# Extra steps of an attention stage at other places in five engines' orders

## The chip, the cores and the metric

The kernel runs on one core of one Trainium2 chip. The metric is the device time of one execution in microseconds (us). An execution that the hardware profiler records has a time of its own; the profile and the trace below are of that one execution. Engines: PE is TensorE, DVE is VectorE, ACT is ScalarE, POOL is GpSimd, SP is SyncE, which here only issues DMAs. Each engine works through a queue of its own in order; they are tied together by semaphores alone.

## The reference

For x of 8 sequences x 256 tokens x 512 features, all in float32:

```
x = x + stack(layernorm(x))        # projection to 64, 4 layers of convolution and a small MLP, projection to 512
x = x + ffn(layernorm(x))          # 512 -> 1792 (gate, up) -> 512, weights w * (su @ sv), SiLU
x = x + attention(layernorm(x))    # below
x = x + ffn(layernorm(x))          # the same weights again
```

The attention has 32 heads of 128 in 8 groups of 4 that share one key and value head:

```
q, k, v = x @ Wq.T, x @ Wk.T, x @ Wv.T            # per head
q, k = rmsnorm(q), rmsnorm(k)
scores = q @ k.T / sqrt(128) + slope[head] * (key - query)   # causal: later keys get -1e30
out = softmax(scores) @ v                          # per head
return concat(out) @ Wo.T
```

## The kernel before

Everything is written by hand for the five queues. Three phases follow one another; the change touches the second, the attention (`order2` and the functions that carry it out), and not the planners of the first and third.

**Units.** The attention stage has 64 units, one per group g (0 to 7) and sequence b (0 to 7), u = 8 g + b. Unit u attends: scores (`sc`, 4 heads), bias and maximum (`bias`, DVE), exponential (`exp`, ACT), reciprocal sum (`rsum`, DVE), scaling of the probabilities (`norm`, POOL, L2446), transposes (`pT`, PE), their split into a high and a low part (`pThi` ACT L2395, `pTlo` DVE L2551), values (`at`), split of the output (`oThi`, `oTlo`, L2556), output product (`outa`, `out`) and residual sum into x (`oadd`, DVE L2561). Beside it the same unit makes q, k and v of unit u + 1: seven products (`qkv`, a Strassen-like scheme), their sums on DVE (`u2` L2455, `u3`, `c22`, `c11`, `u4`, `c21`, `c12`, one semaphore `c_done`), squares (ACT), the inverse roots (`nrm`, POOL L2414), scaling (`ksc` ACT, `qsc1` POOL L2418, `qsc0` DVE L2489), v's split (`vhi`, `vlo` L2486), transposes of k and q (`kT`, `qT`) and their splits (`qTlo` L2527, `kTlo` L2522). The next unit's `sc0` waits for `kTlo` and `qTlo`.

**Order.** Each engine's order within a unit is a line of names, `UNIT_STEPS` (L1946). Besides these steps some units have extra ones. Names such as `set0`, `set1`, `sums`, `rows` in the lines are places for them, and `besides` (L1960) says which extra step stands at which place in which unit:

- **Statistics** `ln` (3, tile): bn_stats and bn_aggr (`dve_ln`, L1374 and L1377) of the tiles of x that earlier units have finished, for the layer norm of the last phase. Two tiles at DVE's `set1` in units 57 to 60, that is (7,1) to (7,4).
- **Sets of weights.** For each group the q, k, v weights are needed in seven parts: three are quarters of the raw weights, four are sums. For group g + 1 they are made in group g, for g = 1 to 6. SP fetches the raw weights at `set0` of b = 1 (`qf`, L912). POOL makes the four sums at `sums` of b = 2 to 5 (`qcomb`, lines 866 to 878 in `pool_group`), 128 x 768 each, from SBUF to SBUF. ACT writes each part's high half (`qhi`, L892) and DVE its low half (`qlo`, L897, two inputs in SBUF): in b = 2, 3, 4 an even part at `set0` and an odd one at `set1`, in b = 5 the seventh at `set1`. SP saves both halves to DRAM (`qsv`, L916). There is a single buffer `q_parts2`, so each `qhi` waits for the save before it. ACT's `set0` stands ahead of its first `exp`.
- **Last sequences' rows.** The normalised, transposed rows of sequences 6 and 7 and the sums of their quarters are made in group 0: `arow` (DVE), `axT` (PE transposes), `aev` (ACT), `acomb` (POOL, four sums, L1007 to L1012) in unit q - 3, then `ahi` (ACT), `alo` (DVE, L965) and the save `asv` (SP) in unit q - 2. The transposes borrow the PSUM banks of k and q, hence the waits of `pe_sequence` on `c_done` and of `kT` and `qT` on `aev`.

SP loads the next rows' operands (`lx`, `xs<-weff_x`, L2265) at `set0`, behind the save that stands at `sets0`; the load waits for the products of the unit (`qkv_mm`).

Of the kernel before, what the change touches and what calls it, by code (L numbers as in the profile page):

```python
# [15 lines left out]
BATCH, SEQ, DM = 8, 256, 512  # L16
# [13 lines left out]
STILES = SEQ // P  # L30
SC = P + SEQ
UNITS = KVH * BATCH
# [136 lines left out]
def hybrid_block(nc, x_in, win, vecs, b1, w1, w2, wout, bout, ffn_w, lr_long, lr_short, wqkv, wo, qk_w, out, weff_gu, weff_dn, weff_s, weff_q, weff_x):  # L169
    with ExitStack() as ctx:  # L170
# [17 lines left out]
        pe, act, dve, pool, sp = nc.tensor, nc.scalar, nc.vector, nc.gpsimd, nc.sync  # L188
# [779 lines left out]
        def pe_sequence(q, j):  # L968
            if q < SEQS1:
                wait_bank(("axT", q, j))  # L970
            else:

                pe.wait_ge(c_done, summed(q - 2, ("c11", "c21")[j]))
            bank, row = sequence_bank(q, j), sequence_row(q, j)
            pe.wait_ge(a_dve, A_DVE["arow", q, j])
            for k in range(KC):
                ins = pe.transpose(psum[:, bank, k * P:(k + 1) * P], row[:, k * P:(k + 1) * P], ident[:])
            ins.then_inc(a_tile, 1)
# [910 lines left out]
        def sb2(name, shape, dt=F32):  # L1889
# [56 lines left out]
        UNIT_STEPS = {  # L1946
# [13 lines left out]
        def besides(engine, where, u):  # L1960

            g, b = divmod(u, BATCH)
            steps = []

            if where == "set0" and engine == "act" and b == 0:
                steps += [("swo", g, 0), ("swo", g, 1)]
            if where in ("set0", "sums") and engine == "pool" and b == 0:
                steps.append(("swo", g, 0 if where == "set0" else 1))
            if where in ("set0", "set1") and engine == "dve" and b == BATCH - 1 and g + 1 < KVH:
                steps += [("alibi", g + 1, hd) for hd in ((0, 1) if where == "set0" else (2, 3))]  # L1970

            if where == "set1" and engine == "dve":
                if UNITS - 7 <= u < UNITS - 3:
                    steps.append(("ln", (3, STILES * (u - UNITS + 7)), STILES))
            if where in ("set0", "set1") and engine == "dve" and u == 0:
                first_tile = NT - TPB + (2 if where == "set1" else 0)
                steps.append(("ln", (2, first_tile), 2))
            if engine == "pool":
                if where == "sums" and u == 1:
                    steps.append(("inv", 2, NBLK - 1))  # L1980
                if where == "set1" and u in (UNITS - 6, UNITS - 4):
                    steps.append(("inv", 3, (u - UNITS + 6) // 2))

            later_g = g + MADE_AHEAD
            if g and later_g < KVH and b in range(2, 6):
                half = 1 if where[-1] == "1" else 0
                e = 2 * (b - 2) + half if b < 5 else 6
                if where in ("set0", "set1", "sets0", "sets1") and engine in ("act", "dve", "sp") and (b < 5 or half) and \
                        (engine == "sp") == where.startswith("sets"):
                    steps.append(({"act": "qhi", "dve": "qlo", "sp": "qsv"}[engine], later_g, e))  # L1990
                if where == "sums":
                    steps.append(("qcomb", later_g, b - 2))

            fresh = u + 3
            if SEQS1 <= fresh < BATCH:
                steps += {("dve", "set0"): [("arow", fresh, 0)], ("pe", "rows"): [("axT", fresh, 0)],
                          ("act", "rows"): [("aev", fresh, 0)], ("dve", "rows"): [("arow", fresh, 1)],
                          ("pe", "set1"): [("axT", fresh, 1)], ("act", "set1"): [("aev", fresh, 1)],
                          ("pool", "set1"): [("acomb", fresh, 0)]}.get((engine, where), [])
            fresh = u + 2  # L2000
            if SEQS1 <= fresh < BATCH and where in ("set0", "rows", "set1") and engine in ("act", "dve"):
                steps.append(({"act": "ahi", "dve": "alo"}[engine], fresh, ("set0", "rows", "set1").index(where)))
            if SEQS1 <= fresh < BATCH and where == "sets1":
                steps.append(("asv", fresh, 0))

            if engine == "sp" and where == "set0":
                if b == BATCH - 2 and g + 1 < KVH:
                    steps += [("lqw", g + 1, j) for j in range(7)] + [("lwo", g + 1, 0)]
                if u + 3 < UNITS and u + 3 not in range(SEQS1, BATCH):
                    steps.append(("lx", u + 3, 0))  # L2010
                if g and later_g < KVH and b == 1:
                    steps.append(("qf", later_g, 0))
                if u == UNITS - 4:
                    steps.append(("load", 0, 0))
            return steps

        def unit_steps(engine, u):
            for name in UNIT_STEPS[engine].split():
                if name in SUMS2:
                    step_ = ("sum", u + 1, name)  # L2020
                elif name in ("set0", "set1", "sums", "rows", "sets0", "sets1"):
                    if u >= 0:
                        yield from besides(engine, name, u)
                    continue
                else:
                    step_ = (name[:-1], u + (name[:-1] in PROJECTING), int(name[-1]))
                assert step_[0] in PROJECTING or step_[0] in ATTENDING

                done = step_[1] == 0 and step_[0] in ("qkv", "prcopy", "sum", "sqr", "nrm", "ksc", "qsc", "vhi", "vlo")
                if 0 <= step_[1] < UNITS and not done:  # L2030
                    yield step_
# [38 lines left out]
        def summed(n, name):  # L2070
            return len(SUMS2) * n + SUMS2.index(name) + 1
# [521 lines left out]
        def pe_phase2():  # L2593
            for what, a, b in order2["pe"]:
# [5 lines left out]
                    pe_projection(a, b)  # L2600
                elif what == "kT":
                    pe.wait_ge(k_sc, a + 1)
                    if SEQS1 <= a + 2 < BATCH:
                        pe.wait_ge(a_act, A_ACT["aev", a + 2, 0])
                    pe.wait_ge(c_done, summed(a, "c11"))
                    for t in range(STILES):
                        ins = pe.transpose(psum[:, KV, t * P:(t + 1) * P], cc[:, t, 0, 0:HD], ident[:])
                    ins.then_inc(kT_mm, 1)
                elif what == "qT":
                    pe.wait_ge(q_sc1 if b else q_sc0, a + 1)  # L2610
                    if b == 0 and SEQS1 <= a + 2 < BATCH:
                        pe.wait_ge(a_act, A_ACT["aev", a + 2, 1])
                    pe.wait_ge(c_done, summed(a, "c12" if b else "c21"))
                    for hd in range(GRP):
                        ins = pe.transpose(psum[:, QB[b], hd * P:(hd + 1) * P], q_heads(b)[:, hd // 2, hd % 2, :], ident[:])  # L2615
# [329 lines left out]
```

## Time and profile before

| | |
|---|---|
| runs shown | 2433.47, 2441.58, 2434.09 us (median 2434.09) |
| the profiled execution | 2437.14 us, span 2435.8 us |
| PE busy | 2373.6 us, 97% of the span |
| DVE, ACT, POOL busy | 1646.2, 1189.8, 800.6 us |
| units of the attention stage | from 684.4 us to about 2000 us, 64 of some 20 to 23 us |
| data moved | 444.85 MB, 183 GB/s on average |

The span is the time from the first to the last instruction of the profiled execution; its own time has 1.3 us around it. Busy time is the time in which an engine carries out an instruction; register, branch, semaphore and DMA-issuing instructions do not count. A unit's length is read as the distance between two first score products (`psum<-kT,qT_h`). A row of the windows view gives a stretch of the span (from:to), its length, the busy time of PE, PEld (weight loads), DVE, ACT and POOL in it with their instructions, the granted clock of PE (1.00 is full speed), the DMA engines' share and GB/s. A row of the timeline gives start, duration, engine, line, operation, output<-inputs, shapes, and in brackets the idle time of the engine before it and what ended it.

### The profile page before, as it was taken

The page shows a single profiled execution, that of the slowest core. Times are in us where ns is not written, and L with a number is a line of the kernel's source. Part 1 is how long each engine was busy: PE and PEld are TensorE (multiplying, and loading weights), DVE is VectorE, ACT ScalarE, POOL GpSimd, SP SyncE. Part 2 cuts the span into 40 slices and gives each one's busy share as a digit, 9 for nine tenths or more (in the row PEclk, how much of TensorE's full clock was granted, in tenths as well). Part 3 has the DMA queues.
Part 4 walks back from the last instruction along what each step waited for, and adds up shares of the span by engine and source line. Part 5 has one row for each costly group of instructions (what it writes and reads, how often), then busy time and mean ns, then how long its engine had stood idle before and what let it go on. Part 6 is the DMA issues. An engine that isn't in the chain of part 4 may idle for free.

```text
span 2435.8 us, 40875 instructions
## 1 busy us (share of the span) xinstructions
PE 2373.6 (97%) x12810; PEld 2020.9 (83%) x12810; DVE 1646.2 (68%) x3961; ACT 1189.8 (49%) x3788; POOL 800.6 (33%) x1204
## 2 busy tenths in 40 slices
PE   6899999999999999999999999999999989999999
PEld 4577777788888888988989889889898878888887
DVE  7666664534277877777777777777777776565553
ACT  6433332233256666666666666666666562222112
POOL 5530343212034344444443444444434350011000
PEclk9899999999999999999999999999999999999999
DMA  4235458987830634535346335344462306555554
GB/s 144 98 134 188 185 206 293 347 334 285 313 122 31 259 118 158 213 147 198 151 173 231 121 153 212 143 183 173 169 238 92 113 19 232 195 208 185 193 193 156
DMA packets 86579, 444.85 MB, mean 183 GB/s; under 512 B 9496, under 2 KB 16664, under 8 KB 66656
## 3 DMA queue, kind: packets, MB, share of 16 engines
q1 hardware_dynamic: 85008, 440.78, 48.5%
q8 instruction: 108, 1.77, 0.3%
q10 hardware_dynamic: 1360, 1.46, 0.2%
q14 instruction: 103, 0.84, 0.1%
HBM read 342.59 MB, written 99.61 MB: 182 GB/s over the span
## 4 chain that ended last, share of the span: by engine, by line
PE 82%; DMA 7%; DVE 4%; POOL 3%; ACT 2%; issue 2%; SPq 0%; ACTq 0%; POOLq 0%; DVEq 0%
PE psum L801 70%; DMA stage<-in_wqkv 3%; PE psum L2639 3%; PE psum L2615 2%; DMA weff_s<-short_st 1%; DMA weff_q<-q_parts 1%; POOL rr L2414 1%; PE psum L2633 1%; POOL prob L2446 1%; PE psum L1793 1%; DVE cc L2489 1%; PE psum L1814 1%; POOL srstd L1184 1%; PE psum L1826 1%; ACT prob L2388 1%
## 5 line engine op out<-in xcount | busy, mean ns | idle before, releaser
L801 PE MATMUL psum<-qw,xs 128*128 128x384 f32 x2688 | 512.0, 340 | 1.7 <-DMA xs<-weff_x 1.7
L801 PEld LDWEIGHTS psum<-qw,xs 128*128 128x128 f32 x2688 | 462.3, 189 | 2.5 <-DMA xs<-weff_x 1.9
L2446 POOL TENSOR_SCALAR prob<-prob,rsum 128x128 f32<-128x128 f32 (+1 forms) x512 | 231.6, 468 | 613.3 <-DVE rsum L2548 608.2
L2388 ACT ACTIVATE prob<-biased,nmax 128x256 f32<-128x256 f32 (+1 forms) x512 | 227.3, 447 | 125.8 <-DVE nmax L2538 125.8
L801 PE MATMUL psum<-wo_h,oT_h 128*128 128x512 f32 x512 | 214.3, 419 | 0.2
L801 PE MATMUL psum<-wo_h,oT_l 128*128 128x512 f32 x512 | 202.7, 396 | 0.0
L801 PE MATMUL psum<-wo_l,oT_h 128*128 128x512 f32 x512 | 202.5, 395 | 0.0
L2334 ACT ACTIVATE squares<-cc 128x128 f32<-128x128 f32 x512 | 152.6, 302 | 52.6 <-DVE cc L2468 49.6
L2489 DVE TENSOR_TENSOR cc<-cc,rr 128x512 f32<-128x512 f32 x64 | 97.7, 1526 | 102.3 <-POOL rr L2414 102.3
L2414 POOL TENSOR_TENSOR rr<-ss,mneg_half 128x6 f32<-128x6 f32 (+1 forms) x128 | 150.3, 1174 | 10.7
L801 PE MATMUL psum<-xT0h,wgu 128*128 128x512 f32 x448 | 152.1, 399 | 0.0
L2551 DVE TENSOR_TENSOR pT_l<-psum,pT_h 128x384 fp32r<-128x384 f32 x256 | 136.1, 552 | 22.9 <-ACT pT_h L2395 15.5
L801 PE MATMUL psum<-xT1h,wgu 128*128 128x512 f32 x448 | 147.3, 394 | 0.0
L801 PE MATMUL psum<-xw_h,wS 128*128 128x512 f32 x448 | 147.1, 389 | 0.0
L2395 ACT ACTIVATE pT_h<-psum 128x384 fp32r<-128x384 f32 x256 | 113.2, 489 | 59.4 <-PE psum L2639 58.4
L801 PE MATMUL psum<-kT,qT_h 128*128 128x256 f32 x512 | 114.5, 305 | 5.6 <-DVE kT L2522 5.6
L2639 PE MATMUL psum<-ident,prob 128*128 128x128 f32 x768 | 109.1, 275 | 9.0 <-POOL prob L2446 8.8
L2556 DVE TENSOR_TENSOR oT_l<-psum,oT_h 128x512 fp32r<-128x512 f32 x128 | 87.6, 684 | 43.8 <-ACT oT_h L2400 43.4
L801 PEld LDWEIGHTS psum<-wo_h,oT_h 128*128 128x128 f32 x512 | 96.2, 188 | 23.8 <-DVE oT_l L2556 4.7
L801 PEld LDWEIGHTS psum<-wo_h,oT_l 128*128 128x128 f32 x512 | 96.2, 188 | 23.0
L1420 DVE TENSOR_TENSOR d<-gate,psum 128x512 f32<-128x512 f32 x56 | 38.4, 686 | 112.2 <-PE psum L801 75.5
L801 PE MATMUL psum<-xw_h,wA 128*128 128x512 f32 x336 | 112.7, 389 | 1.4 <-issue 1.4
(338 smaller groups left out, 5903.0 us busy)
## 6 DMA issues: line engine op xcount, KB each, us to landing
xs<-weff_x SPq DMA_DIRECT2D x62, 1792.0 KB, 7.9
wgu<-weff_gu SPq DMA_DIRECT2D x42, 1024.0 KB, 7.9
weff_q<-q_parts SPq DMA_DIRECT2D x56, 768.0 KB, 3.6
qw<-weff_q SPq DMA_DIRECT2D x56, 768.0 KB, 8.0
wD<-weff_dn SPq DMA_DIRECT2D x56, 512.0 KB, 4.7
wS<-weff_s SPq DMA_DIRECT2D x28, 1024.0 KB, 7.0
wdn<-weff_dn SPq DMA_DIRECT2D x42, 512.0 KB, 4.1
weff_gu<-wgu SPq DMA_DIRECT2D x14, 1024.0 KB, 4.2
```

What stands on the lines that cost most here:

```text
L801: ins = pe.matmul(out_ap, stat[a], mov[b], start=start and n == 0, stop=stop and n == last)
L1420: dve.tensor_tensor(F["d"][:], F["gate"][:, a % 2, :], psum[:, UP, :], ALU.mult).then_inc(d_done, 1)
L2334: ins = act.activation(squares[:, first_place + hd, :], cc[:, tile, half, (hd + 1) * HD:(hd + 2) * HD], ACT.Square, accum_out=ss[:, n:n + 1])
L2388: act.activation(prob[:, b, lo:hi], biased[:, b % 2, lo:hi], ACT.Exp, bias=nmax[:, b, t:t + 1], scale=-1.0, accum_out=esum[:, b, t:t + 1]) ...
L2395: act.activation(pT[0][:, b % 2, :], psum[:, b, 0:SC], ACT.Copy).then_inc(pT_hi, 1)
L2414: pool.tensor_tensor(rr[:, part], ss[:, part], mneg_half[:, 0:part.stop - part.start], ALU.pow).then_inc(r_done, 1)
L2446: pool.tensor_scalar(prob[:, b, lo:hi], prob[:, b, lo:hi], rsum[:, b, t:t + 1], 1.0, ALU.mult, ALU.mult).then_inc(prob_done, 1)
L2489: dve.tensor_tensor(q_heads(0), *q_scaled(0), ALU.mult).then_inc(q_sc0, 1)
L2551: dve.tensor_tensor(pT[1][:, b % 2, :], psum[:, b, 0:SC], pT[0][:, b % 2, :].bitcast(F32), ALU.subtract).then_inc(pT_lo, 1)
L2556: dve.tensor_tensor(oT[1][:, hs, :], psum[:, 2 * b, :].rearrange("p (h c) -> p h c", h=2), oT[0][:, hs, :].bitcast(F32), ALU.subtract).the ...
L2615: ins = pe.transpose(psum[:, QB[b], hd * P:(hd + 1) * P], q_heads(b)[:, hd // 2, hd % 2, :], ident[:])
L2639: ins = pe.transpose(psum[:, b, k * P:(k + 1) * P], prob[:, b, k * P:(k + 1) * P], ident[:])
```

## The change

It changes places only; no instruction is added or removed. There are two new places on DVE, `wait0` (before u2) and `wait1` (before qsc0). The statistics go there, one tile each. The even `qlo` go from `set0` (behind c21) to `wait0`. POOL's `qcomb` goes from `sums` (between norm1 and norm2) to `set0` (before norm0). The rows of sequences 6 and 7, with their transposes, evictions and sums, go one unit earlier (unit q - 4), and the waits that guard their banks with them.

```diff
--- before.py
+++ after.py
@@ -970,7 +970,7 @@
                 wait_bank(("axT", q, j))
             else:
 
-                pe.wait_ge(c_done, summed(q - 2, ("c11", "c21")[j]))
+                pe.wait_ge(c_done, summed(q - 3, ("c11", "c21")[j]))
             bank, row = sequence_bank(q, j), sequence_row(q, j)
             pe.wait_ge(a_dve, A_DVE["arow", q, j])
             for k in range(KC):
@@ -1946,8 +1946,8 @@
         UNIT_STEPS = {
             "pe": "sc0 sc1 sc2 sc3 qkv1 qkv7 qkv6 pT0 pT1 qkv5 qkv2 qkv4 at0 qkv3 rows pT2 pT3 outa0 at1 set1 outa1 kT0 qT1 qT0 "
                   "out0 out1",
-            "dve": "bias0 bias1 rsum0 bias2 rsum1 bias3 u2 pTlo0 u3 pTlo1 c22 c11 rsum2 rsum3 u4 c21 set0 oTlo0 c12 rows pTlo2 "
-                   "pTlo3 qsc0 oTlo1 set1 vlo0 qTlo1 qTlo0 kTlo0 oadd0 oadd1",
+            "dve": "bias0 bias1 rsum0 bias2 rsum1 bias3 wait0 u2 pTlo0 u3 pTlo1 c22 c11 rsum2 rsum3 u4 c21 set0 oTlo0 c12 rows "
+                   "pTlo2 pTlo3 wait1 qsc0 oTlo1 set1 vlo0 qTlo1 qTlo0 kTlo0 oadd0 oadd1",
             "act": "set0 exp0 exp1 exp2 prcopy0 pThi0 pThi1 exp3 sqr5 sqr2 oThi0 sqr4 rows pThi2 pThi3 sqr3 ksc0 oThi1 vhi0 set1 qThi1 "
                    "kThi0 qThi0",
             "pool": "set0 norm0 norm1 sums norm2 norm3 nrm1 nrm0 qsc1 set1",
@@ -1969,9 +1969,8 @@
             if where in ("set0", "set1") and engine == "dve" and b == BATCH - 1 and g + 1 < KVH:
                 steps += [("alibi", g + 1, hd) for hd in ((0, 1) if where == "set0" else (2, 3))]
 
-            if where == "set1" and engine == "dve":
-                if UNITS - 7 <= u < UNITS - 3:
-                    steps.append(("ln", (3, STILES * (u - UNITS + 7)), STILES))
+            if where in ("wait0", "wait1") and UNITS - 7 <= u < UNITS - 3:
+                steps.append(("ln", (3, STILES * (u - UNITS + 7) + int(where[-1])), 1))
             if where in ("set0", "set1") and engine == "dve" and u == 0:
                 first_tile = NT - TPB + (2 if where == "set1" else 0)
                 steps.append(("ln", (2, first_tile), 2))
@@ -1985,13 +1984,13 @@
             if g and later_g < KVH and b in range(2, 6):
                 half = 1 if where[-1] == "1" else 0
                 e = 2 * (b - 2) + half if b < 5 else 6
-                if where in ("set0", "set1", "sets0", "sets1") and engine in ("act", "dve", "sp") and (b < 5 or half) and \
-                        (engine == "sp") == where.startswith("sets"):
+                if where in {"act": ("set0", "set1"), "dve": ("wait0", "set1"), "sp": ("sets0", "sets1")}.get(engine, ()) and (
+                        b < 5 or half):
                     steps.append(({"act": "qhi", "dve": "qlo", "sp": "qsv"}[engine], later_g, e))
-                if where == "sums":
+                if engine == "pool" and where == "set0":
                     steps.append(("qcomb", later_g, b - 2))
 
-            fresh = u + 3
+            fresh = u + 4
             if SEQS1 <= fresh < BATCH:
                 steps += {("dve", "set0"): [("arow", fresh, 0)], ("pe", "rows"): [("axT", fresh, 0)],
                           ("act", "rows"): [("aev", fresh, 0)], ("dve", "rows"): [("arow", fresh, 1)],
@@ -2018,7 +2017,7 @@
             for name in UNIT_STEPS[engine].split():
                 if name in SUMS2:
                     step_ = ("sum", u + 1, name)
-                elif name in ("set0", "set1", "sums", "rows", "sets0", "sets1"):
+                elif name in ("set0", "set1", "wait0", "wait1", "sums", "rows", "sets0", "sets1"):
                     if u >= 0:
                         yield from besides(engine, name, u)
                     continue
@@ -2600,16 +2599,16 @@
                     pe_projection(a, b)
                 elif what == "kT":
                     pe.wait_ge(k_sc, a + 1)
-                    if SEQS1 <= a + 2 < BATCH:
-                        pe.wait_ge(a_act, A_ACT["aev", a + 2, 0])
+                    if SEQS1 <= a + 3 < BATCH:
+                        pe.wait_ge(a_act, A_ACT["aev", a + 3, 0])
                     pe.wait_ge(c_done, summed(a, "c11"))
                     for t in range(STILES):
                         ins = pe.transpose(psum[:, KV, t * P:(t + 1) * P], cc[:, t, 0, 0:HD], ident[:])
                     ins.then_inc(kT_mm, 1)
                 elif what == "qT":
                     pe.wait_ge(q_sc1 if b else q_sc0, a + 1)
-                    if b == 0 and SEQS1 <= a + 2 < BATCH:
-                        pe.wait_ge(a_act, A_ACT["aev", a + 2, 1])
+                    if b == 0 and SEQS1 <= a + 3 < BATCH:
+                        pe.wait_ge(a_act, A_ACT["aev", a + 3, 1])
                     pe.wait_ge(c_done, summed(a, "c12" if b else "c21"))
                     for hd in range(GRP):
                         ins = pe.transpose(psum[:, QB[b], hd * P:(hd + 1) * P], q_heads(b)[:, hd // 2, hd % 2, :], ident[:])
```

## Rows read from the trace of the kernel before

**Rows 1.** Page, busy time of each engine.

```profile
PE 2373.6 (97%) x12810; PEld 2020.9 (83%) x12810; DVE 1646.2 (68%) x3961; ACT 1189.8 (49%) x3788; POOL 800.6 (33%) x1204
```

**Rows 2.** Page, the chain that ended last, by engine.

```profile
PE 82%; DMA 7%; DVE 4%; POOL 3%; ACT 2%; issue 2%; SPq 0%; ACTq 0%; POOLq 0%; DVEq 0%
```

**Rows 3.** Windows: (0,3), (0,4), (0,5); (7,1) to (7,5); (7,5); (7,6).

```profile
749.37:770.44 21.07, 20.91 (x130) 19.12 (x128) 16.24 (x46) 14.12 (x52) 10.49 (x17) 1.00 0.00 1
770.44:793.57 23.13, 21.10 (x129) 18.96 (x128) 19.33 (x51) 15.34 (x55) 11.34 (x17) 1.00 0.08 33
793.57:814.49 20.92, 20.19 (x120) 18.41 (x121) 17.46 (x49) 13.63 (x52) 7.54 (x13) 1.00 0.45 174
...
1857.73:1961.86 104.13, 102.37 (x601) 91.26 (x600) 80.69 (x236) 62.09 (x245) 37.85 (x69) 1.00 0.23 84
...
1941.49:1961.86 20.37, 20.36 (x120) 18.41 (x121) 15.59 (x45) 12.41 (x49) 7.03 (x13) 1.00 0.02 6
...
1961.86:1982.07 20.21, 20.21 (x122) 18.29 (x120) 15.14 (x44) 12.44 (x49) 7.03 (x13) 1.00 0.08 19
```

**Rows 4.** Windows, sum over the six units b = 2 of groups 1 to 6.

```profile
sum 125.94, PE 123.34 PEld 108.85 DVE 97.61 ACT 83.50 POOL 57.75; mean PE 20.56 PEld 18.14 DVE 16.27 ACT 13.92 POOL 9.63
```

**Rows 5.** Windows, b = 3 and 4: (3,3) with (3,4); sum over six pairs.

```profile
1243.56:1284.08 40.52, 40.52 (x241) 36.51 (x241) 33.26 (x93) 27.78 (x102) 19.25 (x28) 1.00 0.44 170
...
sum 248.88, PE 245.51 PEld 218.53 DVE 199.32 ACT 166.79 POOL 115.52; mean PE 40.92 PEld 36.42 DVE 33.22 ACT 27.80 POOL 19.25
```

**Rows 6.** Timeline, kTlo at the end of (7,2); windows, (7,3).

```profile
1899.00 0.47 DVE L2522 SCALAR_TENSOR_TENSOR kT<-psum,kw,kT 128x256 fp32r<-128x256 f32 x1
...
1899.53:1920.52 20.99, 20.55 (x120) 18.24 (x120) 16.38 (x49) 12.41 (x49) 7.04 (x13) 1.00 0.25 89
```

**Rows 7.** Waits, attention stage: sum us, times, longest.

```profile
DVE cc L2489 <- POOL rr L2414: 102.3, 63, 1.7
```

**Rows 8.** Groups by form, attention stage: busy us, mean ns of one, idle before.

```profile
L1374 DVE BATCH_NORM_STATS2 ln_bn<-x 128x6 f32<-128x512 f32 x12 | 8.0, 670 | 0.0
```

**Rows 9.** Timeline, u2 of (2,3): start, us, [idle before <-releaser].

```profile
1086.14 0.55 DVE L2455 TENSOR_TENSOR su<-pr,psum 128x384 f32<-128x384 f32 x1 [0.76 <-PE psum L801]
```

**Rows 10.** Timeline, qhi of (4,4), begun 1427.76; landing of odd saves, (4,3) and (2,5).

```profile
1430.87 0.85 ACT L892 ACTIVATE q_parts<-qt 128x768 fp32r<-128x768 f32 x1 [4.91 <-DMA weff_q<-q_parts]
...
DMA to landing us min/median/max: 5.1/5.1/5.1
...
DMA to landing us min/median/max: 3.2/3.2/3.2
```

**Rows 11.** Timeline, front of (2,2): its qhi and its first norm.

```profile
1062.14 0.85 ACT L892 ACTIVATE q_parts<-stage 128x768 fp32r<-128x768 f32 x1 [4.30 <-DMA stage<-in_wqkv]
...
1064.17 0.83 POOL L2446 TENSOR_SCALAR prob<-prob,rsum 128x128 f32<-128x128 f32 x2 [8.66 <-DVE rsum L2548]
```

**Rows 12.** Timeline, first phase, qcomb and qlo beside each other.

```profile
441.11 1.86 POOL L866 TENSOR_TENSOR qt<-stage 128x768 f32<-128x768 f32 x1 [14.67 <-DMA stage<-in_wqkv]
441.94 1.83 DVE L897 TENSOR_TENSOR q_parts<-stage,q_parts 128x768 fp32r<-128x768 f32 x1 [3.41 <-ACT q_parts L892]
442.92 2.56 POOL L870 TENSOR_TENSOR qt<-stage 128x768 f32<-128x768 f32 x1
```

**Rows 13.** Timeline, end of (2,3) and the first score product of (2,4).

```profile
1095.51 1.04 POOL L2418 TENSOR_TENSOR cc<-cc,rr 128x512 f32<-128x512 f32 x1
...
1095.58 1.53 DVE L2489 TENSOR_TENSOR cc<-cc,rr 128x512 f32<-128x512 f32 x1 [1.67 <-POOL rr L2414]
...
1097.63 0.94 DVE L897 TENSOR_TENSOR q_parts<-qt,q_parts 128x768 fp32r<-128x768 f32 x1
...
1098.49 0.41 DVE L2486 TENSOR_TENSOR v_l<-cc,v_h 128x256 fp32r<-128x256 f32 x1
...
1100.03 0.47 DVE L2522 SCALAR_TENSOR_TENSOR kT<-psum,kw,kT 128x256 fp32r<-128x256 f32 x1
...
1100.67 0.41 PE L801 MATMUL psum<-kT,qT_h 128*128 128x256 f32 x2
```

## The prediction

> **What bounds the kernel now.** I read the page's busy times first: PE is busy for 97% of the span, DVE for 68%, POOL for 33% [rows 1]. The chain that ended last says the same: 82% of it is PE [rows 2]. So work taken off DVE, ACT or POOL is worth nothing by itself; only stretches in which PE waits can change. The changed steps lie in the attention stage alone. I cut it into its 64 units, written (g, b) for group and sequence, each from its first score product to that of the next. An ordinary unit lasts 20.21 us with PE busy throughout, at a granted clock of 1.00 [rows 3]. The longer ones are those with extra steps:
> - units (0,3), (0,4), (0,5), with the last sequences' rows: 21.07, 23.13 and 20.92 us [rows 3];
> - b = 2 of groups 1 to 6, with the first steps of a set of weights: 125.94 us for six [rows 4];
> - b = 3 and 4 of the same groups: 248.88 us for six pairs. An undisturbed pair takes 40.52 (two of the six do) [rows 5];
> - (7,1) to (7,4), with the statistics: with their successor (7,5) 104.13 us for five units, of which (7,5) is 20.37 [rows 3].
>
> **Part 1, statistics.** Eight bn_stats/bn_aggr pairs leave the place before vlo0, one pair each goes to wait0 (before u2) and wait1 (before qsc0). Nothing is added or removed. Today they push vlo, both qTlo and kTlo, for which the next unit's first score product waits: kTlo ends at 1899.47 and the unit begins at 1899.53, 0.06 later [rows 6]. At the new places DVE idles. Before qsc0 it waits 63 times for POOL's reciprocal roots, 102.3 us in all or 1.6 each [rows 7]. Before u2 it idled 0.76 even in a unit whose exponentials stood behind a qhi [rows 9], and these units have none. A pair is about 0.85 us (12 bn_stats take 8.0 us [rows 8], and an aggregation). Both places hold it; without that cover a pair would cost its 0.85. The gain is 104.13 - 5 x 20.21 = **3.08 us**.
>
> **Part 2, last sequences.** Rows, transposes, evictions and sums of sequences 6 and 7 go one unit earlier, to (0,2) and (0,3); their splits and saves stay in (0,4) and (0,5). So (0,4) loses its second load. Each unit then has the load of one that the trace shows: (0,2) and (0,3) that of today's (0,3), 21.07; (0,4) and (0,5) that of today's (0,5), 20.92. Before: 20.21 + 21.07 + 23.13 + 20.92 = 85.33; after: 83.98. Gain **1.35 us**. The transposes' waits on the product sums move with them (three sequences back), so PE waits for nothing newer.
>
> **Part 3, DVE's even splits.** In b = 2, 3, 4 the first qlo (0.94 us) goes from behind c21 to before u2. Its source is ready: ACT's qhi stands before the exponentials, which DVE has used by then. In (2,3) DVE idles 0.76 before u2 [rows 9], so u2 starts about 0.2 late; the product that waits for the sum after it is two products away. In a b = 2 unit less is idle there; u2 goes some 0.6 late. I take nothing, for the same reason, and 6 x 0.6 = 3.6 us as the upper end. The save of the part behind it on SP's queue then starts some 5 us earlier, and no longer runs beside the load of xs. ACT's wait at the start of b = 3 and 4 is for the **odd** part's save: it landed 5.1 us after its issue, and qhi could only start at 1430.87, 3.1 us into its unit, after 4.91 idle; with nothing beside it (b = 5) a save landed in 3.2 [rows 10]. With xs out of the way I take 3.3 for all. This start is then some 1.4 us into the unit, where (in the undisturbed pairs) it cost nothing. The gain is 248.88 - 6 x 40.52 = **5.76 us**; the bounds are 0 and 5.76.
>
> **Part 4, POOL's sums (qcomb).** Four for each of six groups go from between the units' second and third norm to before the first. For b = 2 the sum waits for the raw weights, which landed at about 1062.14; 1.86 later [rows 12] is 1064.00, before the first norm at 1064.17 [rows 11]. So nothing, with 6 x 0.3 = 1.8 us as upper bound. What b = 2 loses today, the wait of 4.30 for that load ahead of qhi [rows 11], stays.
>
> For b = 3 and b = 5 POOL is free right after qsc1 of the **preceding** unit, and nothing holds the sum there. That is where DVE has two instructions with both inputs in SBUF: qsc0 and the odd qlo. The trace shows what such a meeting does. A qlo that starts at 441.94 beside a qcomb ends at 443.77, 1.83 instead of 0.94, which is 0.80 after the qcomb's end at 442.97; the next qcomb in turn ends at 445.48, 1.71 after the qlo [rows 12]. qsc0 likewise ends 0.56 after qsc1 [rows 13]. One engine stands still until the other has finished. By these rows, in b = 2 and b = 4: qsc0 ends at 1097.11, the new qcomb at 1098.82, and the qlo that asks at 1097.63 at 1099.62 instead of 1098.57 [rows 13], **1.05 us late**. vlo, qTlo and kTlo follow without a gap. kTlo ends 0.17 before the next unit, of which 0.06 is needed [rows 13, 6]. PE thus waits 0.94; a unit entered like this is 0.16 longer too (20.37 against 20.21 [rows 3]), since the residual sums are late. 12 x 1.10 = **13.2 us lost**; bounds 12 x (1.05 - 0.17) = 10.6 and, with the qcomb at its full 1.86 and qlo at 0.94 behind it, 12 x 1.4 = 16.8.
>
> The Trainium skill, "SBUF — State Buffer", section "Who interferes with whom", says the same against this change: a DVE instruction with two SBUF inputs and a GpSimd one that reads SBUF exclude each other for a whole instruction. If the two engines shared bandwidth instead, this term would be near 0 and the sum a gain.
>
> For b = 4's sum the wait is for the odd qlo of b = 3. The following vlo starts at 1098.49, before that qlo has ended at 1098.57 [rows 13], so vlo goes first and POOL waits.
>
> **Sum.** -3.08 - 1.35 - 5.76 + 13.2 = +3.0 us. The profiled execution took 2437.14 us (span 2435.8), which would become 2440.1; the median of the runs shown, 2434.09, becomes **2437.1**. A measurement here can tell about 0.5%, 12.2 us, from no change.
>
> **Rivals.**
> 1. The ports do not meet (POOL's sum is late, or qlo slips in first). For it: nothing in the attention stage of before shows a qlo beside a qcomb. Against: rows 12. Then -10.2: 2423.9 us. Chance 0.15.
> 2. The late save stays: the odd qlo is 1.05 later, its save too, and if it still takes 5.1, ACT starts as late as today. The gain of 5.76 is gone: +8.8, 2442.9 us. For it: 5.1 in rows 10; against: xs landed by then. Chance 0.15.
> 3. Slower: in b = 3 POOL's sum gets the port before vlo. vlo then ends some 1.8 us late, and six units lose 1.8 + 0.16 - 0.11 = 1.85 each, 11.1 on top: 2448.2 us. It decides whether qcomb starts before vlo; that needs a release faster than DVE's own next instruction. Chance 0.08.
> 4. The steps move, but their units give nothing back: 2434. Chance 0.04.
>
> My forecast has 0.58. The range 2423 to 2445 takes in the forecast with its bounds (10.6 to 16.8 for the port), rivals 1, 2 and 4. Faster by over 0.5% (below 2421.9) needs rival 1 and a gain in b = 2 too: 0.07. Slower by over 0.5% (above 2446.3) is rival 3, or rival 2 with the upper bounds: 0.10. Between: 0.83.
>
> **What would show it.** (7,1) to (7,4) near 20.3 us each; (0,4) near 20.9; b = 3 units near 20.4, their qhi 1.4 us after the start; in b = 2 and b = 4 of groups 1 to 6 a qlo of about 2.0 us, kTlo's end directly before the next score product, and units near 22.0 (b = 2) and 21.2 (b = 4). I am wrong if that odd qlo stays at 0.95 us, if vlo grows to 2 us in b = 3, or if qhi at the start of b = 3 and 4 still idles 4.9 us for weff_q [rows 10].

## The result, and the profile after

The changed kernel took **2439.39 us** in the median of 20 runs (2436.37 to 2443.08), the kernel before 2434.44 us in 20 runs (2429.45 to 2441.58). The ratio is **1.0020, with a 95% interval of 1.0013 to 1.0027**: 4.9 us slower (3.2 to 6.6), which is less than the 0.5% that the prediction took as its bound. Forecast were 2437.1 us and no change by that bound. In a second comparison, in another batch of runs, the same kernel stood at 1.0013 (1.0004 to 1.0021), 3.2 us slower.

The page after, its busy times and its chain by engine (against [rows 1, 2]):

```profile
PE 2373.6 (97%) x12810; PEld 2025.4 (83%) x12810; DVE 1658.1 (68%) x3961; ACT 1189.8 (49%) x3788; POOL 793.1 (33%) x1204
...
PE 85%; DVE 5%; DMA 4%; POOL 3%; issue 2%; ACT 2%; SPq 0%; DVEq 0%; POOLq 0%; ACTq 0%
```

As a summary this tells little: the same engine is busy for the same share. The answer is in the units. First the attention stage as a whole, windows over its 63 complete units, the kernel before and then after (the columns are the length, busy times of PE, PEld, DVE, ACT and POOL, the granted clock, DMA share and GB/s):

```profile
684.39:1982.07 1297.68, 1284.68 (x7577) 1152.81 (x7577) 1015.24 (x2882) 834.79 (x3157) 555.23 (x873) 1.00 0.42 159
```

```profile
687.57:1986.67 1299.10, 1285.17 (x7577) 1155.30 (x7578) 1027.24 (x2882) 834.27 (x3157) 547.27 (x873) 1.00 0.41 159
```

The same 2882 DVE instructions now take 12.0 us more. Only places changed, so some of these instructions must stand still within themselves. Then the units that the change touches, in windows of the kernel after: (0,4), (0,2) to (0,5) together, (2,2), (2,3), (2,4), and (7,1) to (7,5):

```profile
773.95:794.73 20.78, 20.07 (x121) 18.29 (x120) 17.15 (x49) 14.14 (x53) 7.54 (x13) 1.00 0.08 34
...
731.78:815.49 83.71, 81.95 (x498) 74.77 (x496) 66.98 (x188) 55.23 (x208) 36.07 (x60) 1.00 0.20 75
...
1061.55:1083.34 21.79, 20.66 (x122) 18.02 (x120) 17.03 (x46) 13.90 (x51) 11.10 (x15) 1.00 0.42 165
1083.34:1103.72 20.38, 20.38 (x120) 18.34 (x121) 16.77 (x47) 13.88 (x51) 8.91 (x14) 1.00 0.45 172
1103.72:1124.90 21.18, 20.41 (x122) 18.17 (x121) 17.56 (x47) 13.91 (x51) 9.26 (x14) 1.00 0.41 159
...
1865.41:1966.47 101.06, 101.05 (x601) 91.40 (x600) 82.04 (x236) 62.10 (x245) 38.60 (x69) 1.00 0.24 87
```

The sums over the six units b = 2, over the six pairs b = 3 and 4, and over the six units b = 5 of groups 1 to 6, after:

```profile
sum 131.13, PE 124.24 PEld 108.25 DVE 102.26 ACT 83.39 POOL 66.68; mean PE 20.71 PEld 18.04 DVE 17.04 ACT 13.90 POOL 11.11
...
sum 249.60, PE 244.96 PEld 219.03 DVE 205.65 ACT 166.72 POOL 109.09; mean PE 40.83 PEld 36.51 DVE 34.28 ACT 27.79 POOL 18.18
...
sum 122.37, PE 122.35 PEld 110.18 DVE 95.22 ACT 78.85 POOL 42.17; mean PE 20.39 PEld 18.36 DVE 15.87 ACT 13.14 POOL 7.03
```

Against [rows 3 to 5] and the units of before: the statistics' units went from 104.13 to 101.06 us, the last sequences' four from 85.33 to 83.71, b = 2 from 125.94 to 131.13, the pairs from 248.88 to 249.60, and b = 5 to 122.37 from

```profile
sum 121.57, PE 121.55 PEld 109.40 DVE 94.44 ACT 78.84 POOL 52.97; mean PE 20.26 PEld 18.23 DVE 15.74 ACT 13.14 POOL 8.83
```

before. Gains of 3.07 and 1.62 us stand against losses of 5.19, 0.72 and 0.80. (The stage as a whole is only 1.4 us longer here, less than the runs' 4.9: the pairs of the kernel before took more in its one profile than they usually do, as further profiles below show.)

The loss is at the end of b = 2 and b = 4, where one pattern recurs in all twelve. The timeline at the end of (2,4), after (start, duration, engine, line, tiles, and in brackets the idle time before with what ended it):

```profile
1118.82 1.04 POOL L2417 TENSOR_TENSOR cc<-cc,rr 128x512 f32<-128x512 f32 x1
1118.88 1.52 DVE L2488 TENSOR_TENSOR cc<-cc,rr 128x512 f32<-128x512 f32 x1 [1.63 <-POOL rr L2413]
...
1119.82 2.29 POOL L878 TENSOR_TENSOR qt<-stage,qt 128x768 f32<-128x768 f32 x1
...
1120.93 1.99 DVE L897 TENSOR_TENSOR q_parts<-qt,q_parts 128x768 fp32r<-128x768 f32 x1
...
1122.84 0.41 DVE L2485 TENSOR_TENSOR v_l<-cc,v_h 128x256 fp32r<-128x256 f32 x1
...
1124.37 0.47 DVE L2521 SCALAR_TENSOR_TENSOR kT<-psum,kw,kT 128x256 fp32r<-128x256 f32 x1
1124.90 0.51 PE L801 MATMUL psum<-kT,qT_h 128*128 128x256 f32 x2 [0.76 <-DVE kT L2521]
```

Read it by ends. qsc1 on POOL ends at 1119.86 and qsc0 on DVE, beside it, at 1120.40. POOL's next instruction is the moved qcomb: it ends 1.71 after qsc0. The odd qlo asks at 1120.93 and ends at 1122.92, 0.81 after the qcomb's end at 1122.11; alone it takes 0.94. These are the 1.71 and 0.80 of [rows 12]. vlo, the rest of DVE's chain and kTlo follow without a gap; kTlo ends at 1124.84 and PE, which has idled 0.76 us, begins the next unit at 1124.90.

Over all of the attention stage the groups by form show the same (count, busy time and mean ns): the twelve odd qlo of b = 2 and 4, at 1.98 to 2.00 us, lift the means from 946 and 963 ns before (12 x 1.05 = 12.6 us, against the 12.0 that DVE is busy longer) to

```profile
L897 DVE TENSOR_TENSOR q_parts<-qt,q_parts 128x768 fp32r<-128x768 f32 x24 | 29.3, 1220 | 0.0
...
L897 DVE TENSOR_TENSOR q_parts<-stage,q_parts 128x768 fp32r<-128x768 f32 x18 | 24.0, 1334 | 0.0
```

For rival 3, the end of (2,3) after:

```profile
1100.67 0.94 DVE L897 TENSOR_TENSOR q_parts<-qt,q_parts 128x768 fp32r<-128x768 f32 x1
1101.54 0.42 DVE L2485 TENSOR_TENSOR v_l<-cc,v_h 128x256 fp32r<-128x256 f32 x1
1101.79 1.89 POOL L874 TENSOR_TENSOR qt<-qt,stage 128x768 f32<-128x768 f32 x1 [2.19 <-DVE q_parts L897]
```

POOL waits 2.19 us for the odd qlo, and DVE's own next instruction, vlo, goes first and takes its ordinary 0.42. The sum that starts at 1101.79 beside it ends at 1103.68, again 1.72 after DVE's instruction. Rival 3 did not come about. The waits of the attention stage after (sum in us, times, longest):

```profile
DVE cc L2488 <- POOL rr L2413: 98.6, 63, 1.7
...
ACT q_parts L892 <- DMA weff_q<-q_parts: 43.3, 12, 4.0
...
ACT q_parts L892 <- DMA stage<-in_wqkv: 26.6, 6, 4.7
...
POOL qt L874 <- DVE q_parts L897: 13.1, 6, 2.2
```

The first is now 98.6 against 102.3 [rows 7]: statistics fill part of it. The longest wait of a qhi for a save is 4.0 instead of 4.91 [rows 10]. Rival 2 would have kept it.

### The profile page after: what moved, and what is told of

Same layout as the page of the kernel before. It is cut to its first block, busy times and chain, and to the rows that moved or that the text cites. A ratio compares the mean times of both kernels' runs of the same rounds, so it can differ in the third digit from the quotient of the medians.

```text
span 2438.9 us, 40875 instructions
## 1 busy us (share of the span) xinstructions
PE 2373.6 (97%) x12810; PEld 2025.4 (83%) x12810; DVE 1658.1 (68%) x3961; ACT 1189.8 (49%) x3788; POOL 793.1 (33%) x1204
## 4 chain that ended last, share of the span: by engine, by line
PE 85%; DVE 5%; DMA 4%; POOL 3%; issue 2%; ACT 2%; SPq 0%; DVEq 0%; POOLq 0%; ACTq 0%
PE psum L801 73%; PE psum L2638 3%; DMA stage<-in_wqkv 3%; PE psum L2614 2%; POOL rr L2413 1%; PE psum L2632 1%; DVE q_parts L897 1%; PE psum L1793 1%; DVE cc L2488 1%; PE psum L1814 1%; PE psum L1826 1%; PE psum L2633 1%; PE psum L1784 1%; DVE qT_l L2526 1%; POOL srstd L1184 1%
## 5 line engine op out<-in xcount | busy, mean ns | idle before, releaser
L2445 POOL TENSOR_SCALAR prob<-prob,rsum 128x128 f32<-128x128 f32 (+1 forms) x512 | 217.3, 440 | 562.7 <-DVE rsum L2547 556.8
L2488 DVE TENSOR_TENSOR cc<-cc,rr 128x512 f32<-128x512 f32 x64 | 97.7, 1526 | 98.6 <-POOL rr L2413 98.6
L801 PE MATMUL psum<-kT,qT_h 128*128 128x256 f32 x512 | 116.3, 309 | 11.9 <-DVE kT L2521 11.9
```

The source lines that it names most:

```text
L801: ins = pe.matmul(out_ap, stat[a], mov[b], start=start and n == 0, stop=stop and n == last)
L2445: pool.tensor_scalar(prob[:, b, lo:hi], prob[:, b, lo:hi], rsum[:, b, t:t + 1], 1.0, ALU.mult, ALU.mult).then_inc(prob_done, 1)
L2488: dve.tensor_tensor(q_heads(0), *q_scaled(0), ALU.mult).then_inc(q_sc0, 1)
```

## The experiments

The theory: each of the four parts acts alone in its own units; three save, and the qcomb's exclusion with the odd qlo costs about 13 us. The main rival: the loss has another source (the even qlo before u2, or the earlier requests for transposes), and the long qlo costs nothing. The first four kernels apply one part of the change each to the kernel before, and share one batch of runs of it (27 runs, median 2432.89 us).

**The statistics alone.** The kernel before with only

```
-                   "pTlo3 qsc0 oTlo1 set1 vlo0 ..."      +  "... bias3 wait0 u2 ... pTlo3 wait1 qsc0 ..."
-            if where == "set1" and engine == "dve":
-                if UNITS - 7 <= u < UNITS - 3:
-                    steps.append(("ln", (3, STILES * (u - UNITS + 7)), STILES))
+            if where in ("wait0", "wait1") and UNITS - 7 <= u < UNITS - 3:
+                steps.append(("ln", (3, STILES * (u - UNITS + 7) + int(where[-1])), 1))
```

> The kernel before, with the statistics alone at wait0 and wait1. Theory (they sat on the path of kTlo, and both new places are idle time of DVE): units (7,1) to (7,5) last 5 x 20.21 = 101.1 us instead of 104.1, nothing else changes, the time is 3.1 us lower (2431.3 against 2434.4). Rival (the places are not idle enough, u2 or qsc0 comes late and PE waits there instead): units of 20.5 us or more, gain under 1.5 us.

Measured: 2428.34 us (9 runs), ratio 0.9974 (0.9962 to 0.9986). (The ratios are not those of the medians: these differ by 4.6 us here, where the ratio gives 6.3.) (7,1) to (7,5):

```profile
1853.05:1954.08 101.03, 101.01 (x602) 91.33 (x601) 82.04 (x236) 62.09 (x245) 38.60 (x69) 1.00 0.24 87
```

104.13 became 101.03 with PE busy throughout; the five units are at 20.21 each. The ratio says 6.3 us (3.4 to 9.3), of which the units that the edit touches show 3.1. Some of the rest may be the pairs b = 3 and 4, which differ from one execution to the next (below); that is not shown.

**The last sequences alone.** The kernel before with `fresh = u + 4` for `u + 3`, and with the waits that go with it (`summed(q - 3, ...)` for the transposes; `A_ACT["aev", a + 3, j]` for kT and qT).

> The kernel before, with the rows of sequences 6 and 7 alone one unit earlier. Theory (the two loads met in (0,4)): units (0,2) to (0,5) last 21.1, 21.1, 20.8 and 20.8 us, 83.7 in all instead of 85.3, time 1.6 us lower. Rival (POOL's four sums at the end of a unit hold up DVE's vlo, so each of the two units gets a late kTlo): (0,2) and (0,3) near 22 us, no gain.

Measured: 2430.92 us (11 runs), ratio 0.9995 (0.9985 to 1.0005). (0,2) to (0,5):

```profile
729.09:812.78 83.69, 81.93 (x497) 74.76 (x496) 66.98 (x188) 55.26 (x208) 36.08 (x60) 1.00 0.20 75
```

That is 1.64 less than the 85.33 before. In single units: 21.09, 21.07, 20.77, 20.76, against 20.20, 21.07, 23.13, 20.92. Such a size is too small for the ratio to tell, but the units repeat it to 0.03 us in every kernel with this edit.

**The even qlo alone.** The kernel before, with DVE's even qlo at `wait0` instead of `set0`:

```
+                if where in {"act": ("set0", "set1"), "dve": ("wait0", "set1"), "sp": ("sets0", "sets1")}.get(engine, ()) and (
+                        b < 5 or half):
```

> The kernel before, with DVE's even qlo alone before u2. Theory (the even save no longer runs beside the load of xs, that load lands at about 19.1 us of its unit, the odd save takes 3.3 us): all units b = 3 and 4 of groups 1 to 6 last 20.3 us, 243.1 us for the six pairs instead of 248.9; b = 2 unchanged at 126 us for six; time 5.8 us lower. Rival (the disturbed pairs come from something else, such as the order of the saves on SP): some pairs stay at 42.7 us.

Measured: 2431.41 us (12 runs), ratio 0.9988 (0.9979 to 0.9998), so 2.9 us faster (0.5 to 5.1; by the medians 1.5). The six pairs b = 3 and 4:

```profile
sum 243.48, PE 243.37 PEld 219.20 DVE 199.29 ACT 166.69 POOL 114.49; mean PE 40.56 PEld 36.53 DVE 33.21 ACT 27.78 POOL 19.08
```

The pairs are at 40.58 each, undisturbed but for one of 40.8, as the prediction had it. The reason that it gave is borne out too: with the even save out of its way, the load of xs took 7.5 us in the mean of the 18 units b = 2, 3 and 4 (8.7 before), and the odd saves landed in 3.4 (4.2 before). u2's later start costs nothing: b = 2 is 124.57 for six, not above the 125.94 of before. But two further profiles of the kernel before, below, show that 248.88 was a high reading of what these pairs took.

**qcomb alone.** The kernel before with

```
-                if where == "sums":
+                if engine == "pool" and where == "set0":
                     steps.append(("qcomb", later_g, b - 2))
```

> The kernel before, with POOL's sums alone ahead of the first norm. Theory (two of four sums per group meet the odd qlo and hold it for 1.05 us): in b = 2 and 4 of groups 1 to 6 the odd qlo takes about 2.0 us, each such unit is 0.9 us longer and its successor 0.13; 12.5 us in all, from which the disturbed pairs' 0 to 5.8 us come off, since the later odd save meets less of the load of xs. Time 7 to 13 us higher. Rival (ports cost nothing, the sums only fill idle time): time unchanged within 2 us, every qlo at 0.95 us.

Measured: 2443.24 us (5 runs), ratio 1.0041 (1.0028 to 1.0054), so 10.0 us slower (6.8 to 13.1): the one part of the four that loses. b = 2, and the pairs:

```profile
sum 131.53, PE 123.94 PEld 108.29 DVE 103.40 ACT 83.46 POOL 71.25; mean PE 20.66 PEld 18.05 DVE 17.23 ACT 13.91 POOL 11.88
...
sum 249.61, PE 245.01 PEld 219.13 DVE 206.00 ACT 166.65 POOL 118.48; mean PE 40.84 PEld 36.52 DVE 34.33 ACT 27.78 POOL 19.75
```

The twelve odd qlo of b = 2 and 4 take 1.98 to 1.99 us here too, with none of the other parts present. All b = 3 units last 20.38 or 20.39 and all b = 4 some 21.2, as in the changed kernel, although the even qlo stands at its old place. The disturbance by a late save is all but gone, as the expectation had allowed. In b = 2 the odd save is issued 1.05 us later behind the load of xs than before, when only 0.3 to 1.3 us of the load are left to run (1.3 to 3.3 before), and lands in 3.2 us in all six (3.3 to 5.1 before). In (4,3) it is issued 6.56 us behind the load, as before (1427.99 after 1421.43; before, 1425.68 after 1419.12), and still lands sooner. The difference is in the load. The landings of the load and of the odd save in (4,3), as the views of these two transfers give them, of the kernel before, then of this one:

```profile
DMA to landing us min/median/max: 10.0/10.0/10.0
DMA to landing us min/median/max: 5.1/5.1/5.1
```

```profile
DMA to landing us min/median/max: 8.7/8.7/8.7
DMA to landing us min/median/max: 4.0/4.0/4.0
```

With a load of 10.0 us, 3.5 of it are still to run when the save is issued; with one of 8.7, 2.2. So the distance between the two issues doesn't set the landing; how long the load still runs beside the save does, for the most part (numbers from all profiles stand below). Why this load is shorter here, with the even save where it was, no run shows.

**Taking away the exclusion, not the step.** The changed kernel, in which two of POOL's sums wait for the odd qlo that is next on DVE, so that DVE has it first:

```
                 if g:
-                    pool.wait_ge(gu_lo, made_before)
+                    pool.wait_ge(gu_lo, made_before + (2 if g >= GROUPS1 else 0))
...
-                pool.wait_ge(gu_lo, made_before + 5)
+                pool.wait_ge(gu_lo, made_before + (6 if g >= GROUPS1 else 5))
```

> The changed kernel, with one more condition for POOL's second and fourth sum of groups 1 to 6: they also wait for the odd qlo of the unit before (a semaphore that counts it), as the third one already does. Theory (the two instructions exclude each other, and whoever starts first delays the other): the sums start at about 18.4 us of b = 2 and 4, the odd qlo is back at 0.94 us, b = 4 lasts 20.3 and b = 2 about 21.0 us, b = 3 and 5 20.3; 12.5 us less than the changed kernel, some 2427. Rival (POOL's sums at the unit's end cost by their memory traffic or by the work behind them, wherever they start): b = 2 and 4 stay near 22 and 21.2 us.

Measured: 2426.45 us (5 runs), ratio 0.9958 (0.9946 to 0.9971) to the kernel before, which in this second batch stood at 2435.58 us (17 runs). The changed kernel itself was repeated in the batch (2438.44 us, below): **two added waits take 12.0 us off it**. The end of (2,4) and the sums of b = 2 and of the pairs:

```profile
1111.02 0.94 DVE L897 TENSOR_TENSOR q_parts<-qt,q_parts 128x768 fp32r<-128x768 f32 x1
...
1112.13 1.88 POOL L878 TENSOR_TENSOR qt<-stage,qt 128x768 f32<-128x768 f32 x1 [2.18 <-DVE q_parts L897]
```

```profile
sum 126.00, PE 123.45 PEld 108.86 DVE 96.77 ACT 83.59 POOL 64.90; mean PE 20.57 PEld 18.14 DVE 16.13 ACT 13.93 POOL 10.82
...
sum 243.62, PE 243.49 PEld 219.15 DVE 199.32 ACT 167.08 POOL 107.12; mean PE 40.58 PEld 36.53 DVE 33.22 ACT 27.85 POOL 17.85
```

qlo is 0.94 us again, and POOL stands 2.18 us at a semaphore instead of 0.58 behind qsc0 (from 1119.82 to 1120.40). Nobody waits for POOL there, so its wait is free and DVE's is not. The rival, that the long qlo costs nothing, falls here: nothing but the order of these two instructions differs.

**The changed kernel with qcomb at its old place** (`if where == "sums":` again):

> The changed kernel with POOL's sums back between the second and third norm (parts 1 to 3 of the change without part 4). Theory: the sum of the three gains, 3.1 + 1.6 + 2 to 5.8 us (the last one differs from execution to execution), 2424 to 2428 us; units b = 3 and 4 at 20.3 us, as with the added wait. Rival (the sums ahead of the norms are needed for something, such as the third norm beside a qlo): units of 20.6 us or more and a time within 2 us of before.

Measured: 2426.59 us (6 runs), ratio 0.9962 (0.9950 to 0.9974). b = 2 took 125.27 us, the pairs 243.59. By the medians it equals the kernel with the waits, 0.1 us apart. So qcomb's early place brings nothing of its own even when it doesn't collide.

**A better place for the even steps.** In the kernel just shown, ACT's even qhi goes behind the exponentials, to a new place between exp3 and sqr5, and the even qlo back to where its source is then ready:

```
-  "act": "... pThi1 exp3 sqr5 ..."
+  "act": "... pThi1 exp3 late0 sqr5 ..."
+                if where in {"act": ("late0", "set1"), "dve": ("set0", "set1"), "sp": ("sets0", "sets1")}.get(engine, ()) and (
```

> As the last one, but the even qhi stands behind the fourth exponential on ACT (where ACT idles 0.8 us for c22) and the even qlo behind c21 on DVE as before the change. Theory (the exponentials were held by qhi, which waited for the raw weights in b = 2 and for the odd save in b = 3 and 4): b = 2 too lasts 20.3 us, four or five us less than the last kernel, some 2420 us, whatever the saves take. Rival (the squares behind qhi on ACT come late, and with them POOL's roots and qsc0): b = 2, 3, 4 near 20.8 us and no gain over the last kernel.

Measured: **2421.48 us** (5 runs), ratio 0.9942 (0.9929 to 0.9955), 14.1 us faster than the kernel before (11.0 to 17.3) and the fastest of all. The sum of b = 2, then of the pairs:

```profile
sum 121.27, PE 121.26 PEld 109.31 DVE 97.88 ACT 83.45 POOL 57.71; mean PE 20.21 PEld 18.22 DVE 16.31 ACT 13.91 POOL 9.62
...
sum 243.20, PE 243.17 PEld 219.13 DVE 199.78 ACT 166.71 POOL 115.27; mean PE 40.53 PEld 36.52 DVE 33.30 ACT 27.78 POOL 19.21
```

b = 2 is now an ordinary unit of 20.21 us. What b = 2 had lost, even at its best, was the wait of [rows 11]: qhi stands ahead of the exponentials and waits for the raw weights. Behind them it waits for nothing, as the timeline of ACT in (2,2), begun at 1053.96, shows:

```profile
1061.61 0.84 ACT L892 ACTIVATE q_parts<-stage 128x768 fp32r<-128x768 f32 x1
1062.55 0.31 ACT L2333 ACTIVATE squares<-cc 128x128 f32<-128x128 f32 x1
```

Two steps moved here, qhi and qlo; that the even qlo's place alone costs nothing was seen above. The even save is late again in this kernel, the load of xs takes 8.5 us in the mean and the odd saves land in up to 4.8, yet no pair is disturbed: a late save costs only while a qhi waits for it ahead of the exponentials.

**The changed kernel again,** as the second batch's own measure of it:

> The changed kernel once more, beside the others on the same chip. Theory (the attention stage is 1 to 2 us longer than in the first profile of before, whose disturbed pairs cost 5.8 us, where those of two other kernels with the same places for these steps cost 1.7 and 4.3): units b = 2 at 21.6 to 22.1, b = 3 and 5 at 20.4, b = 4 at 21.2 us again, time 4 to 6 us above before. Rival (the first profile was an unusual one): units b = 2 and 4 differ by over 0.3 us.

Measured: 2438.44 us (11 runs), ratio 1.0013 (1.0004 to 1.0021). Its units repeat the first profile: b = 2 131.73, pairs 249.45, b = 5 122.29, (7,1) to (7,5) 101.03.

**The kernel before, profiled twice more,** for how far one profiled execution stands for the others:

> The kernel before once more, for its profile. Theory (the disturbed pairs differ from execution to execution, and the first profile had many): unit (0,0) 23.0 to 24.4 us, the six pairs b = 3 and 4 between 244.5 and 248.9 us, most likely under 248, all other units as in the first profile. Rival (the kernel before always loses 5.8 us there, and the two experiments that lost less changed it): 248.5 us or more.

> As the last one, a third profile of the kernel before. Theory: pairs between 244.5 and 248.9 us, another value than in the other two. Rival: 248.5 us or more again.

The sum of the six pairs, in the first of these profiles and in the second:

```profile
sum 246.06, PE 244.56 PEld 218.77 DVE 199.42 ACT 166.91 POOL 115.94; mean PE 40.76 PEld 36.46 DVE 33.24 ACT 27.82 POOL 19.32
```

```profile
sum 246.78, PE 244.99 PEld 218.76 DVE 199.48 ACT 166.92 POOL 115.92; mean PE 40.83 PEld 36.46 DVE 33.25 ACT 27.82 POOL 19.32
```

The other units hold still (b = 2 126.07 and 126.27, b = 5 121.60 and 121.59, (7,1) to (7,5) 104.20 and 104.19). The pairs don't: 248.88 [rows 5], 246.06 and 246.78 here, and 244.78 and 247.45 in the two kernels above that leave these steps alone. The same unit can be disturbed in one execution and not in the next; (4,4), for one, was 21.41, 20.67 and 20.50 us in the three profiles of the kernel before.

The twelve traces together show what the disturbance is. First, the landing of a save: of the 216 odd saves of b = 2, 3 and 4, the 15 issued after the load of xs had landed took 3.2 to 3.3 us; the 33 whose load ran 2.0 to 2.5 us longer took 3.9 to 4.4; the 11 whose load ran 3.0 us longer or more took 4.9 to 5.2. There are a few exceptions: two saves took 4.2 and 4.8 where the load ran only 0.7 to 0.8 longer. Second, the load: its mean over these 18 units is 7.5 us in each of the five kernels with the even save early, and 8.5 to 8.8 in the seven profiles with it late. Third, the price: a unit b = 3 or 4 takes 20.25 to 20.29 us when its even qhi starts less than 1.9 us into it; when it starts later, the unit takes 20.27 plus the time by which that start is behind 2.0, within 0.05 (96 units, in the eight profiles in which qhi stands ahead of the exponentials and no sum meets a qlo). (2,4) of the kernel before is such a unit, with 20.48 for a start at 2.18, and (4,3) another, with 21.32 for 3.06.

## Why the prediction was right, and where its sum was off

The sum gave +3.0 us; +4.9 (3.2 to 6.6) was measured, in the forecast's range and on its side of zero. Part by part:

**Part 1, -3.08: right.** 104.13 became 101.06 in the changed kernel and 101.03 with this part alone. DVE's waits hid both pairs.

**Part 2, -1.35: right in kind, 1.6 in size.** The prediction gave (0,4) and (0,5) the 20.92 of before's (0,5); they take 20.78 and 20.75. (0,2) and (0,3) take 21.09 and 21.08 for a forecast 21.07 each.

**Part 3, -5.76: the mis-sized term.** It was read off one execution, 248.88 less six undisturbed pairs of 40.52. Five profiles with these steps untouched have a mean of 246.8, and with the even qlo moved the pairs take 243.48 (243.59 in the changed kernel without the collision): a gain of 3.3 us where it is alone. Of the 2.5 us too much, 2.1 are that this one execution was disturbed more than the mean, and 0.4 that one pair stays disturbed. The term should have been taken in the middle of its bounds and not at their end. Its mechanism holds: the load of xs is shorter by about 1 us with the even save early, and 3.3 was the mean landing of an odd save in the changed kernel. u2's later start, for which the prediction took nothing and up to 3.6 us as a bound, costs nothing. The qhi of (2,3) did start 1.3 us into its unit in the changed kernel, as the forecast said (1.4), and cost nothing there:

```profile
1084.63 0.85 ACT L892 ACTIVATE q_parts<-stage 128x768 fp32r<-128x768 f32 x1 [3.97 <-DMA weff_q<-q_parts]
```

**Part 4, +13.2: right.** By units, against the same kernel without the early qcomb (125.27, 243.59, 121.67): 131.13 - 125.27 = 5.9, 249.60 - 243.59 = 6.0, 122.37 - 121.67 = 0.7, together 12.6 us. By the medians of the runs it is 11.9 against this kernel (2438.44 and 2426.59) and 12.0 against the one with the two waits (2426.45). Its steps: qlo 1.98 to 2.00 (forecast about 2.0), b = 4 at 21.17 to 21.18 but for one of 21.41 (21.2), b = 2 at 21.86 in the mean (22.0), b = 3 and b = 5 at 20.38 to 20.41, for which 0.16 above 20.21 was forecast. The 21.41 is (4,4), whose qhi starts 2.2 us into it since the odd save of (4,3) takes 4.2 us: the one late save that is left. The Trainium skill's page "SBUF — State Buffer", section "Who interferes with whom", says that the side that issues first holds the shared pair for its whole instruction and the other blocks. The trace agrees: qcomb 1.71 after qsc0's end, qlo 0.81 after qcomb's, and 12 us back when the order is turned.

Parts 3 and 4 don't simply add, since the early qcomb by itself nearly ends the disturbance that Part 3 was to remove. Against the mean of 246.8, the pairs lose 2.8 us with qcomb moved, whether the even qlo is moved (249.60, 249.45) or not (249.61). The change by its units is thus 101.06 - 104.17 = -3.1; 83.70 - 85.33 = -1.6; 131.4 - 126.1 = +5.3 for b = 2 (two profiles of after, three of before); +2.7 for the pairs; +0.7 for b = 5: **+4.0 us**, inside both intervals. The forecast's +3.0 is 1.0 below that: Part 3's term was some 2.5 us too large (5.76 for 3.3). Parts 2 and 4, 0.3 and 0.6 us off the other way, took part of it back, and b = 2 another 0.8: without the early qcomb it takes 125.27 in the changed kernel and 126.1 before. That the sum came nearer than its largest term is luck.

**The rivals.** 1 (the ports don't meet) fell, but the kernel with the two waits is the world that it describes: forecast -10.2 us, measured -10.2 by the ratio (7.1 to 13.2, of 2435.58) and -9.1 by the medians. That agreement is partly luck as well, since the -10.2 contains Part 3's 5.76. 2 (the late save stays) and 3 (POOL gets the port ahead of vlo) fell by the rows above. 4 (nothing given back) fell too: all four parts changed their units.

What stays open is why the load of xs takes 10.0 us in one unit and 8 to 9 in another with the same transfers issued around it, and the 1.5 us (by the medians; 3 by the ratio) that the statistics alone gained beyond their units.

## What to carry to other kernels

A place where an engine is free is not free if its neighbour then has a two-input instruction on SBUF (here 1.05 us at each of twelve meetings): look at what the *other* engine of DVE and POOL does in the same microsecond, and let the engine that nobody waits for be the one that stands (here a wait on a semaphore, 12 us). A step that has to wait for data belongs behind the work that others need, not ahead of it: the even qhi moved past the exponentials gave six units of 20.21 for 20.9, and made late saves harmless in the others. And read a wait that is there in some units only from several executions before its price goes into a sum.

## What was not expected of the hardware

The collision is exact. In the changed kernel and in the kernel with qcomb alone every one of the 24 odd qlo took 1.98 to 2.00 us, and in the changed kernel five of the six pairs b = 3 and 4 repeated at 41.56 or 41.57 us. Other stretches, with no difference in their code, repeat far less closely. The first 50 us of the kernel before and of the kernel after, whose first phase is the same (the clock is the third number from the end):

```profile
0.00:50.00 50.00, 31.18 (x146) 20.20 (x146) 38.00 (x121) 31.52 (x68) 24.57 (x74) 0.94 0.52 152
```

```profile
0.00:50.00 50.00, 26.58 (x144) 17.56 (x146) 37.69 (x120) 30.91 (x66) 24.57 (x74) 0.82 0.52 152
```

The granted clock there was 0.94 and 0.82, each a mean of stretches at the full and at the half level (2.4 and 1.2 GHz), and in the attention stage 1.00 in both. No run shows what sets it. The attention stage began between 681.1 and 688.9 us in the twelve profiles, more than the whole change is worth; the stage itself, cut into units, told differences of 0.1 us.
